# An xDeepFM kernel on one core: seven copied row pairs, an earlier x, a split deep input and a shorter final row

## The reference, cut to what matters

```python
emb = tables[feat_idx, sparse]                       # 512 x 26 x 32
linear_out = lin_sparse_w[feat_idx, sparse].sum(-1) + dense @ lin_dense_w
x0 = xk = emb
for w, bb in ((conv1_w, conv1_b), (conv2_w, conv2_b)):
    hp = einsum('bhd,bmd->bhmd', xk, x0).reshape(-1, h * M, E)
    xn = sigmoid(einsum('oi,bid->bod', w, hp) + bb[None, :, None])
    xk, half = xn[:, :64], xn[:, 64:];  res.append(half)
cin_out = concatenate(res, 1).sum(-1) @ cin_w + cin_b
h1 = tanh(deep_x @ W1 + b1); h2 = tanh(h1 @ W2 + b2); h3 = tanh(h2 @ W3 + b3)
out = linear_out + cin_out + h3 @ deep_w + deep_b + bias
```

## Time and profile before

| | |
|---|---|
| median of 3 runs | 430.91 us (430.17 to 431.34) |
| the profiled execution's own time | 432.29 us |
| its span | 430.4 us |
| granted TensorE clock, mean of the span | 0.992 |
| busy: PE, DVE, ACT, POOL | 413.3, 320.0, 161.0, 167.3 us |
| DMA moved | 64.03 MB |

### The profile page before, as it was taken

The page is one execution under the profiler, slowest core; times in us unless marked ns, Lnnn a source line. Parts: engine busy times, 40 slices in busy tenths (PEclk is TensorE's granted clock), DMA queues, the critical chain, the costliest instruction groups (busy, mean ns, idle before and its releaser), DMA issues. The chain is left out here.

```text
span 430.4 us, 5216 instructions
## 1 busy us (share of the span) xinstructions
PE 413.3 (96%) x1874; PEld 167.6 (39%) x1874; DVE 320.0 (74%) x356; ACT 161.0 (37%) x264; POOL 167.3 (39%) x146
## 2 busy tenths in 40 slices
PE   3978989999999999999999999999999999999997
PEld 1422323333333333333233333333333344886784
DVE  4115799898999799999798998998989895332121
ACT  3073252544544534535253544443543411111011
POOL 6663466664746584675540000000000193870000
PEclk9996999999999999999999999999999999999999
DMA  5357696888786898778887778675856720320000
GB/s 195 82 122 164 168 229 162 194 192 196 177 202 141 200 193 210 173 191 184 191 190 189 178 186 192 163 201 133 213 143 153 177 66 10 114 76 0 0 2 0
DMA packets 38304, 64.03 MB, mean 149 GB/s; under 512 B 19601, under 2 KB 22033, under 8 KB 38278
## 3 DMA queue, kind: packets, MB, share of 16 engines
q1 hardware_dynamic: 34694, 61.93, 58.3%
q0 software_dynamic: 3584, 1.76, 3.3%
HBM read 61.96 MB, written 1.71 MB: 148 GB/s over the span
## 5 line engine op out<-in xcount | busy, mean ns | idle before, releaser
L355 POOL DMA_INDIRECT emb<-in_table,rows x112 | 132.8, 1186 | 86.1 <-DMA emb<-in_table,rows 52.6
L730 DVE TENSOR_TENSOR prod<-ring,xk 128x1024 f32<-128x1024 f32 x112 | 132.7, 1217 | 29.2 <-PE ring L431 14.2
L730 DVE TENSOR_TENSOR copied<-copied,xk 128x1024 f32<-128x1024 f32 x96 | 115.4, 1242 | 0.5
L441 PE MATMUL conv<-prod,w_sb 128*64 128x512 f32 x448 | 112.2, 615 | 0.0
L441 PE MATMUL conv<-copied,w_sb 128*64 128x512 f32 x384 | 91.9, 594 | 1.5 <-DVE copied L730 1.5
L419 PE MATMUL conv<-sq,w_sb 117*64 117x512 f32 x384 | 88.1, 593 | 0.3 <-issue 0.3
L579 ACT ACTIVATE xk<-conv,const_sb 64x512 f32<-64x512 f32 x64 | 43.7, 683 | 97.2 <-PE conv L419 84.1
L376 POOL TENSOR_TENSOR xt_lo<-xt,xt_hi 128x512 fp32r<-128x512 f32 (+1 forms) x7 | 12.8, 1863 | 122.1 <-ACT xt_hi L640 122.1
L568 ACT ACTIVATE sq<-ring 117x512 f32<-117x512 f32 x90 | 48.6, 594 | 29.7 <-PE ring L403 23.5
L441 PEld LDWEIGHTS conv<-copied,w_sb 128*64 128x64 f32 x384 | 26.8, 137 | 57.6 <-issue 45.4
L419 PEld LDWEIGHTS conv<-sq,w_sb 117*64 117x64 f32 x384 | 27.2, 136 | 54.2 <-issue 53.4
(11 more groups left out here) (76 smaller groups left out, 299.2 us busy)
## 6 DMA issues: line engine op xcount, KB each, us to landing
copied<-laid SPq DMA_DIRECT2D x192, 256.0 KB
wpiece<-in_mlp SPq DMA_DIRECT2D x22, 256.0 KB
emb<-in_table,rows POOLq DMA_INDIRECT x112
raw<-laid SPq DMA_DIRECT2D x32, 52.0 KB
laid<-emb SPq DMA_DIRECT2D x16, 96.0 KB
sel_f<-in_sel SPq DMA_DIRECT2D x1, 832.0 KB, 5.7
const_sb<-in_const SPq DMA_DIRECT2D x1, 626.0 KB, 4.2
w_sb<-in_w SPq DMA_DIRECT2D x1, 416.0 KB, 6.3
```

Source lines behind the costliest of these rows:

```text
L355: pool.indirect_dma_start(out=emb[0:n, i, j, :], out_offset=None, in_=table, in_offset=bass.IndirectOffsetOnAxis(ap=rows[0:n, i, j:j + 1], ...
L441: mm = nc.tensor.matmul(conv[i % 2][c * HALF:(c + 1) * HALF, :], w2_sb[:, t, :], prod_of(r)[:, c, :], start=(t == 0), stop=(t == T2 - 1))
L730: nc.vector.tensor_tensor(prod_of(r)[:, :, :].rearrange("p c n -> p (c n)"), left[:, :, :].rearrange("p c n -> p (c n)"), xk[i % 2][:, :, ...
```

## The change

Copies and spreads: tile 5 is copied too, so seven of 13 tiles share the six buffers. `lay_out(i + 3)` follows the second copy of a pass, `fetch(i + 3)` precedes the fifth. `fetch` brings each chunk's x twice, to partitions 0, 32, 64 and 96; `x_high` rounds 122 rows and one `scalar_tensor_tensor` with a column of 0 and 1 makes (0 or 1) x raw - rounded in place, the signs in `sel1` and `sel2` being turned for it. `x_high(1)` stands before `sigmoid(0, 1)` and `x_low(1)` before the first product. Gather 1 does not wait for gather 0. The auxiliary row is computed right after the warm-up matmuls, one fewer than before, and is read by ScalarE. The deep input of pairs 0 to 14 is rounded in ScalarE's pass 14 and subtracted by GpSimd at three points given by counts of products, the last pair's 32 columns on their own; `deep(0, 0)` moves behind group 2. The folds are weighted on VectorE and summed by one two-column matmul, and the result reaches one partition through SP. The last deep tile and all that follows is done in two halves of 256 examples.

```diff
-COPIED = (2, 3, 6, 7, 10, 11)
+COPIED = (2, 3, 5, 6, 7, 10, 11)
 RC = 6
-LAY_AT = 3
-DEEP_AT = 1
+LAY_AT, FETCH_AT = 1, 4
+DEEP_AT = 2
-SPREADS_IN = (((0, 4), (0, 5)), ((0, 8), (0, 9)), ((0, 12), (1, 0)), ((1, 1),))
+SPREADS_IN = (((0, 4),), ((0, 8), (0, 9)), ((0, 12), (1, 0)), ((1, 1),))
-X_LOW_AT, TURN_AT, FOLD1_AT, PIECE_AT = (10, 5), 9, (5, 7), 11
-WARM = 13
+X_LOW_AT, TURN_AT, FOLD1_AT, PIECE_AT = (10, 5), 9, (5, 5), 11
+WARM = 12
...
+        XT = PB * (NPAIR - 1)
+        BH = B // 2
+        cin_ps = ring[2][0:2, 0, 0:NPAIR * CB]
+        half_bank = [MLP_BANKS[(HT - 1) % 2][:, 0:BH], ring[1][:, 0, 0:BH]]
+        row_half = [row_ps[0:1, 0:BH], ring[2][0:1, 1, 0:BH]]
...
-                for c in range(2):
-                    sp.dma_start(raw[i % RX][HALF * c:HALF * c + M, :], laid[i, :, c * CH:(c + 1) * CH])\
+                for at in (0, XLO, HALF, HALF + XLO):
+                    c = at // HALF
+                    sp.dma_start(raw[i % RX][at:at + M, :], laid[i, :, c * CH:(c + 1) * CH])\
                       .then_inc(raw_in[i % RX], 16)
...
                 for k in range(NC):
                     n = NC * i + RC + k
+                    if k == FETCH_AT and i + RX < NPAIR:
+                        fetch(i + RX)
                     if n < NC * NPAIR:
                         copy(n)
                     if k == LAY_AT and i + RX < NPAIR:
                         lay_out(i + RX)
-                if i + RX < NPAIR:
-                    fetch(i + RX)
...
+            sp.wait_ge(cin_copied, 1)
+            for c in range(2):
+                sp.dma_start(cin_row[0:1, :].rearrange("p (i c b) -> p c i b", c=2, b=CB)[:, c],
+                             cin2[c:c + 1, :, :]).then_inc(cin_in, 16)
...
-                if i:
+                if i >= 2:
                     pool.wait_ge(rows_in[(i - 1) % GSEM], ROWS * ((i - 1) // GSEM + 1))
...
+            pool.wait_ge(prod_done, T2 * (NPAIR - 2) + 12)
+            for k in range(3):
+                xt_low(k)
+            pool.wait_ge(prod_done, T2 * (NPAIR - 1) + 4)
+            for k in range(3, 5):
+                xt_low(k)
+            pool.wait_ge(prod_done, T2 * (NPAIR - 1) + 8)
+            for k in range(5, K1):
+                xt_low(k)
+            xt_low_rest()
...
+                pe.wait_ge(tanh_done, n - 1)
+                for h in range(2):
+                    at = slice(h * BH, (h + 1) * BH)
+                    for k in range(kt):
+                        for j, (w, x_) in enumerate(((hi, xh), (lo, xh), (hi, xl))):
+                            mm = nc.tensor.matmul(half_bank[h], w[:, k, mt * P:(mt + 1) * P],
+                                                  x_[:, k, at], start=(k == 0 and j == 0),
+                                                  stop=(k == kt - 1 and j == 2))
...
+            pe.wait_ge(aux_in, 16)
+            nc.tensor.matmul(conv[1][0:1, :], small_sb[:, C_AUX:C_AUX + 1], aux[:, :], start=True, stop=True)\
+              .then_inc(aux_done, 1)
...
-                    nc.tensor.matmul(row_ps[0:1, :], small_sb[:, C_AUX:C_AUX + 1], aux[:, :], start=True, stop=False)
-                    by_c = row_ps[0:1, :].rearrange("p (i c b) -> p c i b", c=2, b=CB)
-                    for k, col in enumerate((C_CIN1, C_CIN2)):
-                        for c in range(2):
-                            nc.tensor.matmul(by_c[:, c], small_sb[:, col + c:col + c + 1],
-                                             fold[:, k, :, :], start=False, stop=False, skip_group_check=True)
+                    pe.wait_ge(cin_step, 2)
+                    nc.tensor.matmul(cin_ps, small_sb[:, C_ONE:C_ONE + 2], fold[:, 0, :, :], start=True, stop=True)\
+                      .then_inc(cin_done, 1)
+            deep_halves(2, MT[2] - 1)
...
+            act.wait_ge(table_set, 1)
+            act.wait_ge(aux_done, 1)
+            nc.scalar.activation(row_sb[:, :], conv[1][0:1, :], ACT.Copy).then_inc(aux_read, 1)
             act.wait_ge(sel_done, 2)
             sigmoid(0, 0)
+            x_high(1)
             sigmoid(0, 1)
-            x_high(1)
...
-                for c in range(2):
-                    at = HALF * c
-                    nc.vector.tensor_tensor(x[i % RX][at + XLO:at + XK, :], raw[i % RX][at:at + M, :],
-                                            x[i % RX][at:at + M, :].bitcast(F32), ALU.subtract).then_inc(x_lo_done, 1)
+                nc.vector.scalar_tensor_tensor(x[i % RX][0:XEND, :], raw[i % RX][0:XEND, :],
+                                               small_sb[0:XEND, C_LOW:C_LOW + 1],
+                                               x[i % RX][0:XEND, :].bitcast(F32),
+                                               ALU.mult, ALU.subtract).then_inc(x_lo_done, 1)
...
+                        if i == 0:
+                            x_low(1)
                         dve.wait_ge(xk_ready, 4 * (i + 1))
...
-                    if i == 0 and t == 1:
-                        x_low(1)
```

132 lines of the change are left out of this document (91 added, 41 removed).

## The result

| | before | after |
|---|---|---|
| median | 431.12 us (430.17 to 431.36, 4 runs) | 426.56 us (426.55 to 427.28, 4 runs) |
| ratio | | 0.9902, 95% interval 0.9884 to 0.9921 |
| the profiled execution, its span | 432.29 us, 430.4 | 427.28 us, 425.2 |
| busy: PE, DVE, ACT, POOL | 413.3, 320.0, 161.0, 167.3 us | 406.2, 312.3, 160.9, 166.6 us |
| DMA moved | 64.03 MB | 74.12 MB |

What follows compares the result with a forecast made beforehand. It took PE to set the beat, 20.00 us per pair, with the start a chain of its own. Terms -6.2 + 2.0 - 3.2 - 0.8 + 0.2 - 2.15 + 0 = -10.15 took the median from 430.91 to 420.8 us; range 416.0 to 427.5.

Steps and rivals of the forecast that it cites:

- the start, -6.2 us: Up to pair 1's first main: it begins at 55.8 instead of 61.99, -6.2 us (ends -3.0 and -7.5).
- Raw 1 is there at 30.0.: Start: pair 1's raw x, fetched at 26.9 with issue ended at 28.4, lands at 30.0 after a 1.6 us flight.
- This takes PE at full clock.: Start: PE's longest rest is 1.7 us at 29.6 instead of 4.68, so its clock does not fall.
- not what it says: Rival, start: x_high(1) finds raw 1 late (33, not 30) and holds back sigmoid(0, 1); gain only 3, 424 us; chance 0.07.
- the prediction's own signs of being wrong: A clock below 1 between 30 and 45, DVE waits on copies in pairs 4 to 9, or a beat above 20.
- transfers eat the start's gain: Rival, pairs 1 to 3: all copies land late, +4.2 on the sum, 425.0 us, at most 427 with clock fallen; chance 0.20.
- Pairs 1 to 3, +2.0: Price in transfers: copy 6 behind fetch 2 and copies behind gather 3 land with no reserve; +2.0 us (0 to +6.2).
- the rival of a DMA bound in every pair: Pairs 1 to 9: at 202 GB/s a pair's 4.33 MB takes 21.4 us against 19.77; 433.7 us; chance 0.05.
- Steady and late pairs, -3.2 and -0.8: Tile 5 unspread saves 0.23 us in each of 14 pairs, -3.2; sooner fetch ends most late pairs, -0.8 (0 to -1.1).
- Pair 15, +0.2: Last pair: subtractions spread over pairs 14 and 15, main 12 ends at 362.1; +0.2 us (-1.9 to +1.4).
- Rows between the deep layers, -2.15: Between deep layers 1 and 2: one two-column matmul replaces the aux and four fold matmuls; -2.15 us (-1.7 to -2.3).
- tail 0: Last deep tile: 24 matmuls of 256 columns for 12 of 512, priced by load spacing; 0 us (-0.3 to +1.6).

Runs made afterwards that it cites:

- e2_sp: Changed kernel with SyncE's start order alone changed: lay_out(1) and fetch(1) ahead of copies 0 and 1; 424.85 us (0.9865).
- e12_gather_wait: Changed kernel with gather 1 waiting for gather 0 again; 426.42 us.
- e1_fill: Changed kernel with four more float32 filler matmuls, results unread, between layer 1 of pair 0's second half and pair 1's sums; 425.76 us (0.9883).
- e15_all: e14_sp_copy6 with the four filler matmuls and 14 warm-up matmuls added; 425.04 us.
- e14_sp_copy6: Changed kernel with SyncE's order of e2_sp and copy 6 between lay_out(2) and fetch(2); 423.88 us (0.9829).
- e13_copy6: Changed kernel with copy 6 (tile (0, 11)) issued between lay_out(2) and fetch(2) instead of behind fetch(2); 425.47 us (0.9857).
- e8_sp_fill_lay: Changed kernel with SyncE's order of e2_sp, four filler matmuls, 14 warm-up matmuls and lay_out(3) behind the fourth copy; 426.19 us.
- e6_deep_early: Changed kernel with deep(0, 0) behind main 7 of pair 15 again and all seven 480-column GpSimd subtractions in pair 14; 427.18 us.
- e9_sp_fill: Changed kernel with SyncE's order of e2_sp, four filler matmuls and 14 warm-up matmuls, lay_out(3) staying behind the second copy; 424.51 us.
- e3_x_order: Changed kernel with pair 1's x rounded behind pair 0's sigmoids again and its low part behind pair 0's second product; 426.91 us.
- e5_no_low: Changed kernel with GpSimd subtracting 8 columns per deep-input tile instead of 480 (or 32), the low part left out, so less exact; 425.12 us.
- e7_lay_late: Changed kernel with lay_out(3) behind the fourth of pair 0's seven copies instead of the second; 429.70 us.
- e16_before_fetch: Kernel before with only lay_out(i+3) moved behind a pair's second copy and fetch(i+3) behind the fourth; 429.67 us (0.9964).
- e4_six: Changed kernel with six copied row pairs again, row pair 5 spread by TensorE; 428.55 us (0.9944).

## Why the prediction was wrong

**The step that failed is the start, -6.2 us, measured -2.53** (-1.41 and -1.29 in the other two executions of the program). Two of its premises were false, and a third, behind them, would have cost much of its worth.

*"Raw 1 is there at 30.0."* It was there at 31.13. The flight was guessed well (1.8 us from the end of the issue at 29.36, for 1.6), but the issue itself came at 27.82 and not at 26.9. The gather's issue moved forward, as the step said, but not its landing: e2_sp, which takes copies 0 and 1 out of its way, has it 2 us sooner (23.57), and in e12_gather_wait the time does not miss the sooner issue. I followed gather 1 through GpSimd's program and not through the DMA engines. The rival "not what it says" (0.07) came nearest, with a raw 1 at 33.

*"This takes PE at full clock."* The clock fell to 0.66 behind a rest of 3.71 us. e1_fill puts that at 1.4 to 2.6 us at pair 1. With the clock held, PE went from the sums of pair 1 to pair 1's first main in 24.8 us (33.29 to 58.08), a wait of 2.77 us of VectorE for a copy included, and in 23.3 without that wait (e15_all, 33.78 to 57.04); the step-through had 24.5 (31.3 to 55.8). The stepping was right to about 1 us, its two premises were not. The clock at 0.66 between 30 and 40 us is also the one of the prediction's own signs of being wrong that came.

*That a sooner pair 1 is a sooner end.* The rival "transfers eat the start's gain" (0.20) had its size, but saw late copies in full engines and not the gathers. (Its "at most 427" is not worked out; 425.0 and the clock's 3.2 make 428.2.) Beside PE runs the path of gathers and copies. Over all kernels with seven copies and `fetch` at its new place, in the order of gather 3's landing (the start of `lay_out(3)`), one execution each:

| kernel | gather 3 landed | pair 1's first main | pair 4's first main | pairs 1 to 3 |
|---|---|---|---|---|
| e14_sp_copy6 | 50.15 | 59.09 | 118.40 | 59.31 |
| e2_sp | 50.78 | 59.48 | 118.79 | 59.31 |
| e13_copy6 | 52.29 | 60.15 | 119.46 | 59.31 |
| e8_sp_fill_lay | 52.61 | 59.31 | 120.58 | 61.27 |
| e15_all | 53.02 | 57.04 | 119.90 | 62.86 |
| after | 54.06 | 59.46 | 121.24 | 61.78 |
| e1_fill | 54.48 | 58.08 | 119.67 | 61.59 |
| e6_deep_early | 54.80 | 60.58 | 119.96 | 59.38 |
| e9_sp_fill | 55.34 | 60.68 | 121.50 | 60.82 |
| e3_x_order | 55.46 | 60.27 | 120.14 | 59.87 |
| e12_gather_wait | 55.48 | 60.63 | 121.45 | 60.82 |
| e5_no_low | 55.91 | 60.70 | 121.68 | 60.98 |
| e7_lay_late | 57.76 | 61.50 | 122.76 | 61.26 |

In the first three rows gather 3 is there 7.9 to 8.9 us before pair 1, pairs 1 to 3 take exactly three beats, and pair 4 follows pair 1. In the other ten it comes at most 6.7 us ahead, and up to 3.6 us are lost in pairs 1 to 3; the two that began pair 1 first (57.04 and 58.08) lost 3.55 and 2.28 of it. So the two paths must move together. Single rows must not be read finer than that: three of them (after, e6_deep_early, e5_no_low) are the same program up to there, and their pair 4 lies 1.7 us apart. Up to pair 4, start and transfers together were forecast at -4.9 (with the beat) and gave -0.95 (-2.23 and -0.51 in the other two executions of the program); e14_sp_copy6 gives -3.79 (122.19 - 118.40), with the clock still fallen, and e15_all, with both premises mended, -2.29. Seventh copy, fetch and start are no terms of a sum: the same fillers gain 0.8 us at most with the sooner fetch and lose 2.7 without.

**Pairs 1 to 3, +2.0, measured 2.5** in the profiled execution, and 0.1 and 1.7 in the other two of the same program. The size agrees with the first by some luck, and the reason was half right: copy 6 behind `fetch(2)` was named, but "no reserve" was read as a matter of what the engines carry. e13_copy6 carries the same bytes at the same share with no wait at all. It is a matter of order, of what lies ahead of a gather and behind a `lay_out`. Gather 2, taken at 39.5, landed at 41.27. The fullness of 1.01 was harmless, as the forecast said of the later pairs: the rival of a DMA bound in every pair has not come, with 229 GB/s over 160 us.

**Steady and late pairs, -3.2 and -0.8.** Right: -3.47 for pairs 4 to 14 against -3.3. e16_before_fetch gives the sooner places 1.4 alone. That they carry the rest of the change (some 10 us) was not seen.

**Pair 15, +0.2, measured +1.41,** the upper end of its bounds, which was worked out as "every copied tile collides". All of them lost something, 1.25 us together, and `deep(0, 0)` no longer filled PE's waits of 0.95 and 0.74 us. e5_no_low gives 1.3 of it to the collision; by e4_six 0.8 go with tile 5 as a copied one, which is no further share of the 1.41. The Trainium skill's lock, which the prediction set against its own value, would have given the right number.

**Rows between the deep layers, -2.15, measured -2.16; tail 0, measured -0.03.** In the changed kernel's timeline of the tail:

```profile
418.24 0.28 PE L514 MATMUL ring<-xt_hi,m_hi 128*128 128x256 f32 x1
418.24 0.19 PEld L514 LDWEIGHTS ring<-xt_hi,m_lo 128*128 128x128 f32 x1
418.36 0.27 PE L514 MATMUL ring<-xt_hi,m_lo 128*128 128x256 f32 x1
418.36 0.19 PEld L514 LDWEIGHTS ring<-xt_lo,m_hi 128*128 128x128 f32 x1
```

Loads and matmuls come 0.12 us apart although each load is recorded at 0.19. As chosen, the spacing prices a load and not its duration; 24 of these take 2.86 us in the chain that ended last, for the 2.76 of 12 full ones before. The shorter last tanh and addition pay for it.

Open: why copy 6, 0.52 MB moved forward by 3.9 us, brings gather 3 in sooner, by 1.8 us and by 2.5 and 3.6 against the other two executions. That copies ahead of a gather delay it was shown (e2_sp, e7_lay_late); how the engines share themselves between the two is not. The Trainium skill, page DMA: Bandwidth & Descriptors, section on queues, rings and completion order, says that an engine goes round its queues packet by packet; no run here shows that. Open too is why e15_all, with early gathers and a held clock, had gather 3 at 53.02 where e14_sp_copy6 had it at 50.15.
